# Four layers on one core: operand addresses modulo 256 bytes, and one half of a weight product streamed apart

## The chip, the core and the metric

The kernel runs on one core of a Trainium2 chip. Its time is the device time of one execution in microseconds. The kernel before takes 638.99 us (median of 3 runs, 638.83 to 639.39).

## The reference, cut to what matters

Four layers, each with a residual, work on x of 8 x 256 tokens and 1024 features, all in float32:

```python
x = x + x @ w_eff.T              # L0: weight quantized with a codebook, plus a rank-64 term
x = x + x @ W1.T + 2 * lora(x)   # L1: 8 experts of rank 16, top-2 gates from x @ Wr.T
x = x + x @ W2.T + b + 2 * (x @ A[id]) @ B[id]   # L2: adapter by batch
x = x + x @ W3[id].T             # L3: a whole 1024 x 1024 weight by batch
```

The first three linear parts do not depend on the batch, so the kernel multiplies them together first: E = (I + W0)(I + W1)(I + W2), with the small matrices of the adapters carried along as further columns.

## The kernel before, in words

A float32 number is held as two numbers of type float32r, a high part and the rest. `product` (lines 1259 to 1263) multiplies two such pairs with three matmuls: high by high, high by low, low by high. In `pe.matmul(out, a, b)`, a is the stationary operand of 128 columns, which a weight load puts into the array, and b is the moving one, which streams through it. Each matmul has a weight load of its own; it runs beside the matmul before it.

**First step (about 10 to 127 us).** W1 times the rows of W2. The moving rows are `e_hi` and `e_lo`, the two halves of `e_both` (8 rows of 2 x 1312 numbers; a half is 5,248 bytes). The stationary tiles are W1's columns in two ring buffers, `ring_hi` and `ring_lo`, with room for two tiles. For each of 8 tiles m there are three chunks of 384, 512 and 256 columns; a chunk is `chunk(n)` (line 1333 on): 8 values of k, one product each, 24 matmuls. Between chunks stand `br(c)` (the same product for the adapters, with `bcat_up` and `bcat_down` in rows 7 and 6 of `e_mid` as stationary tiles) and `lora(u)` (the rank-64 term, four matmuls of 256 columns).

**Second step (127 to 239 us).** W0, which DVE and ACT quantize meanwhile in `beat` rounds, times the result. Moving rows: `e_hi` and `e_mid` (8 rows of ES = 1296 numbers, 5,184 bytes). Stationary: the same rings. Three chunks of 384, 512 and 392 columns for each of 8 tiles.

**Four groups of 512 tokens (239 to 635 us).** `low_rank` (moving: `e_both`, stationary: x), then seven `block_product`s of 48 matmuls with 256 columns (moving: x's parts in `x_both`, `x_pair` and both rings, stationary: E's parts in `e_hi`), with the sums and splits of blocks on DVE and ACT. In `gates` (line 1427 on) 16 times four matmuls of 256 columns: `gt_hi` and `gt_lo` (in `bc_hi` and `bc_lo`) move against `br_hi` and `br_lo`, and `h2_k` (in `e_mid`) moves against `bs_half` (in `bc_hi` and `bc_lo`). Then `y_product`, 192 matmuls of 512 columns: W3's parts in `e_hi` move against x's in `e_mid`.

SP issues nearly all loads in program order. PE, ACT, DVE and POOL follow one plan (`phase1_plan`) for the two steps, and written orders (`group`) for the groups. POOL adds the identities to the weights. PE waits on `ring_down` (a tile of a ring is split), `chunk_out` (a bank of PSUM is read out), `delta_out` (the rank-64 term is read out) and `w3_lo` (a half row of W3 is split).

SBUF tensors lie in the order of their declaration. Counted from the start of `e_both`, the bytes of a partition before are: `e_mid` at 83,968, `x_both` at 125,632, `ring_lo` 158,400, `x_pair` 166,592, `ring_hi` 174,784, `raw` 182,976, `bc_hi` 207,552, `bc_lo` 211,648, `br_hi` 215,808, `br_lo` 220,416.

Of the kernel before, what the change touches and what calls it, by code (L numbers as in the profile page):

```python
# [5 lines left out]
F32 = mybir.dt.float32  # L6
F32R = mybir.dt.float32r
# [5 lines left out]
P = 128  # L13
D = 1024
KT = D // P
NB = 8
# [17 lines left out]
ES = EC + 8  # L34
TW = ER + NE + R2
SLOT = [7 if i == 1 else 3 + i // 2 if i % 2 else i // 2 for i in range(NB)]
# [25 lines left out]
N1 = 3 * KT  # L62

# [86 lines left out]
def build(nc, x, cb, lang, id2, id3, w0, scale_log, lora_a, lora_bt, w1, wrt, at, bcat,  # L150
          w2t, b, las, lbs, w3t, y):
    plan = phase1_plan()
    with ExitStack() as ctx:
# [9 lines left out]
        with ExitStack() as whole:  # L163
            def place(name, shape):
                return whole.enter_context(nc.sbuf_tensor(name, shape, F32))
# [5 lines left out]
            ring_lo_w = place("ring_lo_w", [P, 4, 512])  # L171
# [5 lines left out]
        ring_lo = sb("ring_lo", [P, 4, 512], F32R)  # L177
        x_pair = sb("x_pair", [P, 2, D], F32R)
        ring_hi = sb("ring_hi", [P, 4, 512], F32R)
        raw = sb("raw", [P, RAW, D], F32)  # L180
        tmp = sb("tmp", [P, 4, 512], F32)
# [3 lines left out]
        br_hi = sb("br_hi", [P, A0], F32R)  # L185
        br_lo = sb("br_lo", [P, A0], F32R)

        br_now = sb("br_now", [P, 2, 4 * R2], F32R)
        ident = sb("ident", [P, P], F32)
        wr_raw = sb("wr_raw", [P, KT, NE], F32)  # L190
        bias_col = sb("bias_col", [P, KT], F32)
        scales = sb("scales", [P, 2, KT, NE], F32)
        cbs = sb("cbs", [P, 4], F32)
        thr = sb("thr", [P, NL], F32)
        dif = sb("dif", [P, NL], F32)
# [4 lines left out]
        lbias = sb("lbias", [P, NB, NE], F32)  # L200
        lg = sb("lg", [P, 4, NE], F32)
        mx = sb("mx", [P, 4, 4], F32)
        gw = sb("gw", [P, 6, 4], F32)
        oh = sb("oh", [P, 3, 4, NE], F32)
# [6 lines left out]
        scl, rscl = scales[:, 0, :, :], scales[:, 1, :, :]  # L211


# [35 lines left out]
        h2_k = mid[0:96, 8192:8704]  # L249

        tok = mid_w[:, 8704:8704 + 4 * TW].rearrange("p (t c) -> p t c", t=4)
        bs_raw = mid_w[0:96, 8704 + 4 * TW:9728 + 4 * TW]
        h2_tok = scales[:, :, :, :].rearrange("p a k e -> p (a k e)").rearrange("p (t c) -> p t c", t=4)
        h2_sum = mid_w[0:32, 8704:8704 + TG]
        gt_hi, gt_lo = bc_hi[:, 0:TG], bc_lo[:, 0:TG]
        bs_half = [bc_hi[0:96, TG:D], bc_lo[0:96, TG:D]]
# [75 lines left out]
        s_ident = sem("s_ident")  # L332
        s_iota = sem("s_iota")
# [202 lines left out]
        def _(pool):  # L536
# [5 lines left out]
            for j in range(2):  # L542
                pool.memset(br_now[:, j, :].bitcast(F32), 0.0).then_inc(s_ident, 1)
            pool.wait_ge(s_ident, 4)
# [52 lines left out]

            pool.wait_ge(br_down, 3)
# [10 lines left out]
        def _(act):  # L609
# [21 lines left out]
            def split_ring(i, whole):  # L631
# [7 lines left out]
                act.activation(ring(ring_hi, i)[:, ks, :], whole[:, ks, :], ACT.Copy).then_inc(ring_up, 1)  # L639
# [48 lines left out]
            for item in plan:  # L688
# [8 lines left out]
                elif what == "w1_first":  # L697

                    act.wait_ge(s_w1_first, 16)
                    act.activation(ring(ring_hi, 0)[:, 4:KT, :], w1_raw(0)[:, 4:KT, :], ACT.Copy).then_inc(first_up, 1)  # L700
# [187 lines left out]
        def _(dve):  # L888
# [55 lines left out]
            def split_ring(i, whole):  # L944
                dve.wait_ge(ring_up, i + 1)
                ks = slice(0, KT if i else 4)
                minus(ring(ring_lo, i)[:, ks, :], whole[:, ks, :], ring(ring_hi, i)[:, ks, :]).then_inc(ring_down, 1)
# [68 lines left out]
            for item in plan:  # L1016
                what = item[0]
                if what == "w1_first":
                    dve.wait_ge(first_up, 1)
                    minus(ring(ring_lo, 0)[:, 4:KT, :], w1_raw(0)[:, 4:KT, :], ring(ring_hi, 0)[:, 4:KT, :]  # L1020
                          ).then_inc(first_down, 1)
                elif what == "w1_diag":
                    dve.wait_ge(s_w1[0], 16)
                    dve.wait_ge(s_ident, 4)
# [233 lines left out]
        def _(pe):  # L1258
# [46 lines left out]
            def first_chunk():  # L1305
# [3 lines left out]
                for i, kk in enumerate(W2_ORDER[0]):  # L1309
# [269 lines left out]
```

## Time and profile before

| | us |
|---|---|
| median of 3 runs | 638.99 |
| the profiled execution, its own time | 638.79 |
| its span, first to last instruction | 637.0 |
| PE busy | 631.9 |
| DVE busy | 501.4 |
| ACT busy | 364.7 |
| POOL busy | 90.3 |

Times of the rows are counted from the span's start. A matmul's shown duration holds its way through the array, and successive ones overlap, so what one costs is the distance from its start to the start of the next. Where two start times with a known number of matmuls between them are given, their difference over that number is the cost of one.

### The profile page before, as it was taken

Reading aid. Unit: us, or ns where it says so; the run is one execution under the profiler, and the core shown is the slowest. Engines: PE = TensorE matmul, PEld = TensorE weight load, DVE = VectorE, ACT = ScalarE, POOL = GpSimd, SP = SyncE. Lnnn points to the kernel's source line nnn. Section 1 sums busy time; section 2 is a strip of 40 time slices with the busy share of each in tenths; the row PEclk is TensorE's granted clock in tenths of the full one; section 3 lists DMA queues with packets and bytes.
Section 4 is the critical chain, followed back from the end, with each engine's and each line's share of the span. In section 5 each row is a group of like instructions: output and inputs, shape, how many; then the busy total and the mean of one; then the engine's idle time right before and its main releaser. Section 6 shows DMA issues by size and latency. Waiting matters only on the chain.

```text
span 637.0 us, 10326 instructions
## 1 busy us (share of the span) xinstructions
PE 631.9 (99%) x3992; PEld 584.5 (92%) x3992; DVE 501.4 (79%) x645; ACT 364.7 (57%) x549; POOL 90.3 (14%) x120
## 2 busy tenths in 40 slices
PE   8999999999999999999999999999999999999997
PEld 8899999999999999999889999889999889999886
DVE  6899999879991538988887778888687989686753
ACT  6674583972731336745774746665655765664553
POOL 2210225003210010001220001231001223000120
PEclk9999999999999999999999999999999999999999
DMA  8772112111104001213673222684213485002372
GB/s 285 209 206 75 59 33 67 34 33 34 34 0 133 1 1 34 63 64 101 208 253 125 67 67 68 199 261 161 68 34 100 147 283 190 1 1 67 131 245 86
DMA packets 46020, 67.32 MB, mean 106 GB/s; under 512 B 3604, under 2 KB 32020, under 8 KB 45972
## 3 DMA queue, kind: packets, MB, share of 16 engines
q1 hardware_dynamic: 40900, 58.28, 29.0%
q10 hardware_dynamic: 5072, 8.39, 3.8%
q8 instruction: 31, 0.51, 0.4%
q14 instruction: 17, 0.14, 0.1%
HBM read 58.27 MB, written 8.39 MB: 105 GB/s over the span
## 4 chain that ended last, share of the span: by engine, by line
PE 99%; DVE 0%; POOL 0%; issue 0%; POOLq 0%
PE ps L1263 30%; PE ps L1261 30%; PE ps L1262 30%; PE ps L1406 4%; PE ps L1404 1%; PE ps L1272 1%; PE ps L1434 1%; PE ps L1357 1%; PE ps L1450 0%; PE ps L1462 0%; PE ps L1460 0%; PE ps L1442 0%; DVE tmp L1249 0%; DVE tmp L1251 0%; POOL ident L540 0%
## 5 line engine op out<-in xcount | busy, mean ns | idle before, releaser
L1263 PE MATMUL ps<-e_both,ring_lo 128*128 128x384 f32 (+3 forms) x384 | 133.3, 347 | 0.0
L1261 PE MATMUL ps<-e_both,ring_hi 128*128 128x384 f32 (+3 forms) x384 | 133.1, 347 | 0.0
L1262 PE MATMUL ps<-x_both,e_both 128*128 128x256 f32 x448 | 123.7, 276 | 0.0
L899 DVE TENSOR_TENSOR e_both<-raw,e_both 128x512 fp32r<-128x512 f32 x128 | 90.7, 733 | 28.1 <-ACT e_both L773 27.7
L1262 PE MATMUL ps<-e_both,e_mid 128*128 128x512 f32 (+2 forms) x288 | 109.2, 379 | 0.0
L1261 PE MATMUL ps<-e_both,e_mid 128*128 128x512 f32 (+2 forms) x288 | 109.1, 379 | 0.0
L1263 PE MATMUL ps<-e_both,e_mid 128*128 128x512 f32 (+2 forms) x288 | 109.1, 379 | 0.0
L773 ACT ACTIVATE e_both<-raw 128x512 fp32r<-128x512 f32 x128 | 78.8, 628 | 51.5 <-PE ps L1263 51.2
L589 POOL TENSOR_TENSOR raw<-raw,ident 128x128 f32<-128x128 f32 x64 | 47.3, 741 | 338.8 <-DMA raw<-w_t 338.8
L1262 PEld LDWEIGHTS ps<-x_both,e_both 128*128 128x128 f32 x448 | 84.1, 188 | 0.0
L1263 PEld LDWEIGHTS ps<-e_both,ring_lo 128*128 128x128 f32 x384 | 72.1, 188 | 5.5
L1261 PEld LDWEIGHTS ps<-e_both,ring_hi 128*128 128x128 f32 x384 | 72.2, 188 | 5.5
L1262 PE MATMUL ps<-e_mid,ring_hi 128*128 128x384 f32 (+2 forms) x192 | 68.6, 357 | 0.0
L646 ACT ACTIVATE tmp<-tmp,dif 128x1024 f32<-128x1024 f32 x48 | 54.2, 1150 | 18.9 <-DVE tmp L968 15.0
L1262 PE MATMUL ps<-e_both,ring_hi 128*128 128x384 f32 (+2 forms) x192 | 64.5, 336 | 0.0
L970 DVE SCALAR_TENSOR_TENSOR tmp<-w_w,thr,tmp 128x1024 f32<-128x1024 f32 x48 | 60.5, 1303 | 4.2 <-ACT tmp L646 3.8
L1261 PEld LDWEIGHTS ps<-e_both,e_mid 128*128 128x128 f32 x288 | 54.1, 188 | 10.1
L1262 PEld LDWEIGHTS ps<-e_both,e_mid 128*128 128x128 f32 x288 | 54.1, 188 | 10.0
L1263 PEld LDWEIGHTS ps<-e_both,e_mid 128*128 128x128 f32 x288 | 54.1, 188 | 10.0
L899 DVE TENSOR_TENSOR e_both<-e_both_w,e_both 128x1024 fp32r<-128x1024 f32 (+2 forms) x45 | 51.3, 1174 | 10.2 <-ACT e_both L685 7.8
L1261 PE MATMUL ps<-ring_hi,e_both 128*128 128x256 f32 x192 | 53.4, 278 | 0.0
L1263 PE MATMUL ps<-ring_hi,e_both 128*128 128x256 f32 x192 | 53.0, 276 | 0.0
(175 smaller groups left out, 1264.4 us busy)
## 6 DMA issues: line engine op xcount, KB each, us to landing
raw<-w_t SPq DMA_DIRECT2D x64, 512.0 KB, 4.1
w_w<-x_t SPq DMA_DIRECT2D x16, 512.0 KB, 3.8
w_w<-w SPq DMA_DIRECT2D x15, 512.0 KB, 5.3
y<-tmp ACTq DMA_DIRECT2D x30, 256.0 KB, 3.5
e_both_w<-w_t SPq DMA_DIRECT2D x5, 512.0 KB, 7.8
e_both_w<-w_t SPq DMA_DIRECT2D x4, 384.0 KB, 6.0
e_mid_w<-bs SPq DMA_DIRECT2D x24, 64.0 KB, 3.0
e_mid_w<-b_cat SPq DMA_DIRECT2D x4, 128.0 KB, 5.9
```

The costliest lines, as they stand in the source:

```text
L589: pool.tensor_tensor(d, d, ident[:, :], ALU.add).then_inc(w3_diag, 1)
L646: act.activation(acc[i], acc[i], ACT.Identity, bias=dif[:, LEVELS - 1 - level:LEVELS - level]).then_inc(q_add, 1)
L773: act.activation(w3_ring_hi[(2 * k + h) % 4], raw[:, k % RAW, h * 512:(h + 1) * 512], ACT.Copy).then_inc(w3_hi, 1)
L899: return dve.tensor_tensor(out, whole, hi.bitcast(F32), ALU.subtract)
L970: ins = dve.scalar_tensor_tensor(out=acc[i], in0=qf, scalar=thr[:, k:k + 1], in1=acc[i], op0=ALU.is_gt, op1=ALU.mult)
L1261: pe.matmul(out, a[0], b_[0], start=start, stop=False, **kw)
L1262: pe.matmul(out, a[0], b_[1], start=False, stop=False, **kw)
L1263: return pe.matmul(out, a[1], b_[0], start=False, stop=stop, **kw)
L1272: ins = pe.matmul(ps[:, lora_bank(u), 2 * P * i:2 * P * (i + 1)], stack_b[:, b_cols], (stack_a, stack_al)[low][:, a_cols], start=not low a ...
L1357: pe.matmul(ps[:, 7, 0:P], ident[:, :], ident[:, :], start=True, stop=True)
L1404: pe.matmul(ps[:, 4 + t, 0:TW], x_lo[block][:, k % 4, cols], e_hi[:, k, ecols], start=k == 0, stop=False, skip_group_check=True)
L1406: ins = pe.matmul(ps[:, 4 + t, 0:2 * TW].rearrange("p (h c) -> p h c", h=2), x_hi[block][:, k % 4, cols], e_both[:, k, :, ecols], start=Fa ...
```

## The change

- **Middle rows at 5,376 bytes.** ES grows from EC + 8 to EC + 56 numbers: a row of `e_mid` has 5,376 instead of 5,184 bytes. The small tensors `wr_raw`, `scales`, `thr`, `dif`, `lg`, `lbias`, `mx`, `gw`, `oh`, `br_now` and `h2_tok` move into free columns of `e_mid` and `e_both`; `scales` and `wr_raw` are then 8 rows of 32 bytes in each partition. `h2_k` stands 16 numbers further on.
- **Rings.** `ring_hi` and `ring_lo` become 32 numbers longer. W1's and W0's tiles are written and read at `up` and `down`, which begin 32 numbers (128 bytes) into them; x's operands still begin at their start.
- **High and low rows apart.** Chunks 6 to 23 use `chunk_by_halves`: first all 16 matmuls whose moving rows are of `e_hi`, then the 8 of `e_lo`; in chunks of even number the other way round. The number of matmuls is the same.
- **Gates.** `bc_hi` and `bc_lo` become longer, `bs_half` begins 16 numbers further on, and `ids_sb` stands behind `ident`. The places of `gt_hi`, `gt_lo`, `h2_k`, `br_hi`, `br_lo` and `bs_half` follow from that.
- **br_now** is cleared by POOL behind the last chunk with columns 896 on, no longer at the start; PE's first wait is for two updates of `s_ident` instead of four.

```diff
-ES = EC + 8
+ES = EC + 56
+RING_AT = 32
+H2_AT = KT * D + 16
+TOK_AT = H2_AT + TG
+SMALL_AT = TOK_AT + 4 * TW + D
+BY_HALVES = 6
...
-        ring_lo = sb("ring_lo", [P, 4, 512], F32R)
+        ring_lo_all = sb("ring_lo_all", [P, 4 * 512 + RING_AT], F32R)
+        iota_i = sb("iota_i", [P, NE], I32)
+        iota_f = sb("iota_f", [P, NE], F32)
+        lang_i = sb("lang_i", [P, NB], I32)
+        lang_f = sb("lang_f", [P, NB], F32)
         x_pair = sb("x_pair", [P, 2, D], F32R)
-        ring_hi = sb("ring_hi", [P, 4, 512], F32R)
+        ring_hi_all = sb("ring_hi_all", [P, 4 * 512 + RING_AT], F32R)
         raw = sb("raw", [P, RAW, D], F32)
         tmp = sb("tmp", [P, 4, 512], F32)
-        bc_hi = sb("bc_hi", [P, D], F32R)
-        bc_lo = sb("bc_lo", [P, D], F32R)
-        ids_sb = sb("ids_sb", [1, 2, NB], I32)
+        bc_hi = sb("bc_hi", [P, D + 64], F32R)
+        bc_lo = sb("bc_lo", [P, D + 16], F32R)
         br_hi = sb("br_hi", [P, A0], F32R)
         br_lo = sb("br_lo", [P, A0], F32R)
...
+        ring_hi, ring_lo = [of[:, 0:2048].rearrange("p (a c) -> p a c", c=512) for of in (ring_hi_all, ring_lo_all)]
+        up, down = [of[:, RING_AT:2048 + RING_AT].rearrange("p (a c) -> p a c", c=512)
+                    for of in (ring_hi_all, ring_lo_all)]
...
-        bs_half = [bc_hi[0:96, TG:D], bc_lo[0:96, TG:D]]
+        bs_half = [of[0:96, TG + 16:D + 16] for of in (bc_hi, bc_lo)]
...
+            pool.wait_ge(chunk_mm, chunk_number(1, KT - 1, 2) + 1)
+            pool.memset(br_now[:, :, :].bitcast(F32), 0.0).then_inc(br_clear, 1)
+            pool.wait_ge(br_clear, 1)
             pool.wait_ge(br_down, 3)
             pool.wait_ge(e2_down, 4)
             now(0, True)
...
+            def chunk_by_halves(n):
+                _, m, c = CHUNKS[n]
+                c0, w = LEFT[c]
+                pe.wait_ge(ring_down, m + 1)
...
+                out = ps[:, CHUNK_BANK[n], 0:w]
+                parts = [(e_hi, (up, down)), (e_lo, (up,))]
+                for i, (rows, halves) in enumerate(parts if n % 2 else parts[::-1]):
+                    for k in range(KT):
+                        for a, half in enumerate(halves):
+                            ins = pe.matmul(out, ring(half, m)[:, k, :], rows[:, k, c0:c0 + w],
+                                            start=i == 0 and k == 0 and a == 0,
+                                            stop=i == 1 and k == KT - 1 and a == len(halves) - 1)
+                ins.then_inc(chunk_mm, 1)
```

## Rows read from the trace of the kernel before

**Rows 1.** The page: span, PE's busy time and share, granted clock in 40 slices.
```profile
span 637.0 us, 10326 instructions
...
PE 631.9 (99%) x3992; PEld 584.5 (92%) x3992; DVE 501.4 (79%) x645; ACT 364.7 (57%) x549; POOL 90.3 (14%) x120
...
PEclk9999999999999999999999999999999999999999
```

**Rows 2.** PE's waits: us in total, times, longest.
```profile
PE ps L1357 <- POOL br_now L543: 1.6, 1, 1.6
```

**Rows 3.** Timeline of PE, block product: start, duration in us; 29 matmuls apart.
```profile
283.00 0.28 PE L1262 MATMUL ps<-x_both,e_both 128*128 128x256 f32 x1
...
286.29 0.28 PE L1261 MATMUL ps<-bc_hi,br_hi 128*128 128x256 f32 x1
```

**Rows 4.** Timeline of PE, gates and the start of y; 61 matmuls apart.
```profile
286.63 0.28 PE L1434 MATMUL ps<-e_mid,bc_hi 96*128 96x256 f32 x1
...
293.98 0.40 PE L1261 MATMUL ps<-e_both,e_mid 128*128 128x512 f32 x1
```

**Rows 5.** Timeline of PE, y product; 24 matmuls apart.
```profile
304.89 0.39 PE L1261 MATMUL ps<-e_both,e_mid 128*128 128x512 f32 x1
...
310.33 0.39 PE L1261 MATMUL ps<-e_both,e_mid 128*128 128x512 f32 x1
```

**Rows 6.** Timeline of PE, rank-64 term at the start; 14 matmuls apart.
```profile
8.38 0.40 PE L1272 MATMUL ps<-bc_lo,bc_hi 128*128 128x256 f32 x2
...
10.06 0.40 PE L1272 MATMUL ps<-x_pair,bc_hi 128*128 128x256 f32 x2
```

**Rows 7.** Timeline of PE, first step, tile 3: starts and ends of three chunks.
```profile
60.94 0.34 PE L1261 MATMUL ps<-e_both,ring_hi 128*128 128x384 f32 x1
...
65.10 0.40 PE L1272 MATMUL ps<-bc_lo,bc_hi 128*128 128x256 f32 x2
...
65.58 0.39 PE L1261 MATMUL ps<-e_both,ring_hi 128*128 128x512 f32 x1
...
71.10 0.28 PE L1261 MATMUL ps<-e_both,ring_hi 128*128 128x256 f32 x1
...
73.93 0.28 PE L1272 MATMUL ps<-bc_lo,bc_hi 128*128 128x256 f32 x1
```

**Rows 8.** Timeline of PE, second step, tile 6: starts of its chunks and the next.
```profile
211.03 0.34 PE L1261 MATMUL ps<-e_both,ring_hi 128*128 128x384 f32 x1
...
215.22 0.39 PE L1261 MATMUL ps<-e_both,ring_hi 128*128 128x512 f32 x1
...
220.78 0.34 PE L1261 MATMUL ps<-e_both,ring_hi 128*128 128x392 f32 x1
...
225.05 0.34 PE L1261 MATMUL ps<-e_both,ring_hi 128*128 128x392 f32 x1
```

**Rows 9.** Timelines of DVE, ACT and PE where PE's waits end last.
```profile
45.95 1.21 DVE L899 TENSOR_TENSOR ring_lo<-w_w,ring_hi 128x1024 fp32r<-128x1024 f32 x1
...
47.91 0.34 PE L1261 MATMUL ps<-e_both,ring_hi 128*128 128x384 f32 x1
...
102.89 1.09 ACT L618 ACTIVATE raw<-ps 128x512 f32<-128x512 f32 x2 [9.33 <-DVE w_w L979]
...
105.06 0.40 PE L1272 MATMUL ps<-bc_lo,bc_hi 128*128 128x256 f32 x2
...
505.98 1.56 DVE L899 TENSOR_TENSOR e_both<-raw,e_both 128x512 fp32r<-128x512 f32 x2
...
507.22 0.40 PE L1261 MATMUL ps<-e_both,e_mid 128*128 128x512 f32 x1
```

**Rows 10.** DMA issue of scales (KB, us to landing); ACT and DVE behind it.
```profile
scales<-scale_log SPq DMA_DIRECT2D x1, 32.0 KB, 7.6
...
32.58 1.06 ACT L728 ACTIVATE e_both<-w_w 128x1024 fp32r<-128x1024 f32 x1 [3.37 <-DMA w_w<-as]
...
34.62 1.21 DVE L899 TENSOR_TENSOR e_both<-w_w,e_both 128x1024 fp32r<-128x1024 f32 x1
```

More of the change, by code:

```diff
@@ L248, in build @@
         w3_ring_lo = [e_hi[:, 4 + i, 512:D] for i in range(4)]
[L249 to L254, printed above, removed]
+        h2_k = mid[0:96, H2_AT:H2_AT + TG]
+        tok = mid_w[:, TOK_AT:TOK_AT + 4 * TW].rearrange("p (t c) -> p t c", t=4)
+        bs_raw = mid_w[0:96, TOK_AT + 4 * TW:SMALL_AT]
+        h2_sum = mid_w[0:32, TOK_AT:TOK_AT + TG]
         gt_hi, gt_lo = bc_hi[:, 0:TG], bc_lo[:, 0:TG]
[L256 removed]
+        bs_half = [of[0:96, TG + 16:D + 16] for of in (bc_hi, bc_lo)]
         stack_b, stack_a, stack_al = bc_hi, bc_lo, x_pair[:, 1, :]
@@ L541, in _ @@
                                pattern=[[-1, P]], channel_multiplier=1).then_inc(s_ident, 1)
-            for j in range(2):
-                pool.memset(br_now[:, j, :].bitcast(F32), 0.0).then_inc(s_ident, 1)
-            pool.wait_ge(s_ident, 4)
+            pool.wait_ge(s_ident, 2)
             pool.memset(stack_al[R0:P, :].bitcast(F32), 0.0).then_inc(lora_clear, 1)
@@ L638, in split_ring @@
                 ks = slice(0, KT if i else 4)
-                act.activation(ring(ring_hi, i)[:, ks, :], whole[:, ks, :], ACT.Copy).then_inc(ring_up, 1)
+                act.activation(ring(up, i)[:, ks, :], whole[:, ks, :], ACT.Copy).then_inc(ring_up, 1)
             def beat(p, r):
@@ L699, in _ @@
                     act.wait_ge(s_w1_first, 16)
-                    act.activation(ring(ring_hi, 0)[:, 4:KT, :], w1_raw(0)[:, 4:KT, :], ACT.Copy).then_inc(first_up, 1)
+                    act.activation(ring(up, 0)[:, 4:KT, :], w1_raw(0)[:, 4:KT, :], ACT.Copy).then_inc(first_up, 1)
                 elif what == "lora_first":
@@ L946, in split_ring @@
                 ks = slice(0, KT if i else 4)
-                minus(ring(ring_lo, i)[:, ks, :], whole[:, ks, :], ring(ring_hi, i)[:, ks, :]).then_inc(ring_down, 1)
+                minus(ring(down, i)[:, ks, :], whole[:, ks, :], ring(up, i)[:, ks, :]).then_inc(ring_down, 1)
             def beat(p, r):
@@ L1019, in _ @@
                     dve.wait_ge(first_up, 1)
-                    minus(ring(ring_lo, 0)[:, 4:KT, :], w1_raw(0)[:, 4:KT, :], ring(ring_hi, 0)[:, 4:KT, :]
+                    minus(ring(down, 0)[:, 4:KT, :], w1_raw(0)[:, 4:KT, :], ring(up, 0)[:, 4:KT, :]
                           ).then_inc(first_down, 1)
@@ L1379, in _ @@
             for n in range(1, 2 * N1):
-                chunk(n)
+                if BY_HALVES <= n < N1:
+                    chunk_by_halves(n)
+                else:
+                    chunk(n)
                 if n in BR_AFTER:
```

62 lines of the change are left out of this document (38 added, 24 removed).

## The prediction

> **What bounds the kernel now.** I read the page first: PE is busy for 631.9 of the 637.0 us of the span, and its granted clock is at the full level (2.4 GHz) in all 40 slices [rows 1]. Then the list of PE's waits: it has one entry, 1.6 us ahead of the first warm-up matmul [rows 2]. So no transfer and no other engine ends anything; the time is the sum of the distances between 3,992 matmul starts. The question is what one matmul costs, and for that I read start times far apart.
>
> Block product: 29 matmuls of 256 columns from 283.00 to 286.29, 113.4 ns each [rows 3]. Y product: 24 of 512 columns in 5.44 us, 226.7 ns each [rows 5]. The second is twice the first, 0.4427 ns a column, where 2.4 GHz alone would be 0.4167. I call this the base: 113.3 ns for 256 columns, and by the same slope 170.0 for 384 and 173.5 for 392. Now the others. Gates: the first three matmuls, 286.29 to 286.63, are at base; the next 61 of the same size take 7.35 us, 120.5 ns each [rows 3, 4]. Rank-64 term at the start: 14 in 1.68 us, 120.0 ns [rows 6]. First step, tile 3: 4.16 us for 24 of 384 (173.3 ns), 5.52 for 24 of 512 (230.0), 2.83 for 24 of 256 (117.9) [rows 7]. Second step, tile 6: 4.19, 5.56 and 4.27 us, or 174.6, 231.7 and 177.9 ns [rows 8]. Equal shapes on equal clock differ by up to 7 ns, without any wait.
>
> What differs is addresses. From the order and sizes of the tensors I work out each operand's phase: its address modulo 256 bytes, from the start of e_both. A row of e_both has 10,496 bytes, 41 times 256, and its half 5,248, so e_hi has phase 0 and e_lo 128; column offsets 384 and 896 are whole multiples.
>
> - Block product: moving x's parts, all 192; stationary 0. Moving phase constant, stationary minus moving 64. Base.
> - Y product: both 0, constant, difference 0. Base.
> - Gates: gt_hi and gt_lo 192 against br 0, then h2_k 0 against bs_half 192: the moving phase turns twice in four matmuls. The slow stretch begins with the first h2_k.
> - First step: moving 0, 128, 0; stationary 192. Second: e_hi 0, e_mid's row k at 64k (5,184 is 64 over a multiple); stationary 192. Off base.
> - Rank-64 term: both 192, constant, and yet 6.7 ns over base.
>
> So a constant moving phase with a difference of 64 runs at base, a turning one does not, and constancy alone is not enough. That is the reading on which I forecast.
>
> **The change part by part.** All sums are against the profiled execution, 638.79 us (span 637.0 and 1.8 around it), 0.2 below the median 638.99.
>
> *Gates.* New phases from the new sizes: gt_hi, gt_lo and h2_k 64, br and bs_half 128. Constant, difference 64, 256 columns: the case of the block product. 61 matmuls x 7.2 ns is 0.44 us, four groups 1.76. At the least nothing; I take 1.7, as a turn remains at either end.
>
> *Second step.* A row of 5,376 bytes is 21 times 256, so e_mid has phase 0 like e_hi; the rings go from 192 to 64. Constant, difference 64. Over base now: 4.19 - 4.08 = 0.11, 5.56 - 5.44 = 0.12, 4.27 - 4.16 = 0.11 us a tile. Eight tiles: 1.84 for the first two chunks and 0.86 for the third. The block product shows the rule for 256 columns only, but 384 and 512 are also whole multiples of 64 bytes. 392 is not: its last piece is half of one, and I take half of that chunk's gain, 0.43. For the turn of size at 24 chunk starts I give back 0.01 each: the y product needs 1.39 us for its first six instead of 1.36 when it follows the gates (its start is the last of [rows 4]), which is 0.03 for a turn of phase and size together. 1.84 + 0.43 - 0.24 = 2.0 us. Bounds: 0 and 2.7.
>
> *First step, chunks 6 to 23.* 12.51 us a tile against 12.24 at base [rows 7], so 0.27 a tile, 1.64 for six. By halves, the 16 matmuls of e_hi have moving 0 and stationary 64, the good case; the 8 of e_lo have 128 against 64, a difference of 192, which before occurs only mixed with others. Between 0 and the rank-64 term's 6.7 ns for each of those; I take 4.5, near the mean overrun now (0.27 us / 72 = 3.8 ns). 8 x 4.5 + 10 for the turn is 46 ns a chunk; 18 chunks keep 0.83 and give 0.8 us. Bounds 0.3 and 1.64.
>
> *Chunks 0 to 5, br, the rank-64 term.* The order is as before with other phases; two of three matmuls of a ring product now have a difference of 64, before one of three. br's stationary tiles go to phase 0, the rank-64 term to 64 against 64 and 192. Nine chunks' worth of products, about 90 ns over base each, 0.8 us, and 64 matmuls of the term with up to 0.43. I take a gain of 0.1; bounds +0.5 and -1.2 us.
>
> *low_rank, block products, y product.* Both operands keep their phases: x's parts stay at 192 (32,768, 8,320 + 128 bytes and so on keep it), E's and W3's at 0. Nothing.
>
> *Start.* PE's first wait goes from L543's end to that of the identity, 0.2 to 0.3 us earlier, but warm-up is all that moves; the rank-64 term waits for DVE's split of data from a DMA. Nothing. br_now is cleared while DVE still splits the last columns; POOL then waits for them anyhow. Nothing.
>
> *Small tensors.* scales and wr_raw arrive in runs of 32 bytes instead of 256, 1,024 instead of 128. The load of scales now takes 7.6 us to land in a queue full of W2; ahead of the adapters, whose landing lets ACT start at 32.58. ACT is done at 33.64 and DVE comes for it at 34.62 [rows 10], so up to 0.9 us more costs nothing. Beyond it DVE's chain slips, and PE has 0.75 us to its next ring tile (45.95 + 1.21 = 47.16 against 47.91 [rows 9]). I take 0; the bound is half a microsecond.
>
> *What is late next.* PE comes earlier, and others don't. Tile 2 of the ring has 0.75 us, of which chunks 0 to 5 can use some tenths. The rank-64 unit that PE takes at 105.06 waits for ACT at 102.89 + 0.6 = 103.5 [rows 9], 1.5 us, and ACT waits for DVE there; PE will be 0.7 to 1.2 us early. In the third group W3's half row is split at 505.98 + 0.7 + some hundredths, 506.95, and PE takes it around 507.2 [rows 9]: that is almost bound, by x's transfers. With gates 0.44 us shorter it can cost 0.2 once. I take 0.2 in all.
>
> Sum: 1.7 + 2.0 + 0.8 + 0.1 - 0.2 = 4.4 us; 638.79 - 4.4 = 634.4.
>
> Rows against a page: matmuls alike in shape take 113.4 and 120.5 ns within one microsecond of each other [rows 3, 4]. The Trainium skill (TensorE: Matmul & The Clock Gate, Part 2, the step on LDWEIGHTS) says that PE has two independent read ports and that loading the next weights takes nothing from the running matmul; by that no address could matter and the sum would be 0, the third rival. The same page (Back-to-back issue gap) gives N / 2.4 + 2.5 ns, 109.2 for 256 columns by its formula, an estimate that no row here reaches. The measurement decides against both as written, though not on why.
>
> **The rivals.**
>
> 1. *All at base.* The halves of e_lo and the 392 columns run clean too, and the early products gain. 1.76 + 2.7 + 1.64 + 0.9 = 7.0, so 631.8. For it: y runs clean with another difference (0). Against: the rank-64 term doesn't.
>
> 2. *Only part holds.* The difference 64 helps at 256 columns as shown, longer ones or e_lo keep most of their overrun: gates 1.7 and a third of the two steps' 4.3 make 3.1 less 0.2, or only the gates 1.7. 635.9 to 637.1. For it: in the second step rows k = 0 and 4 of e_mid already have e_hi's phase and the chunks are still off base, though with difference 192.
>
> 3. *The addresses are not the cause.* Something in the alternation of tensors or banks is. The change then does not do what it says; 638.8, with 0.2 either way. Against it stands the break in the gates after three matmuls.
>
> 4. *Slower: the new constant phases lock into the bad pattern.* The rank-64 term shows that a constant pair can cost 6.7 ns for every matmul without end. If the rings at 64 do that, 42 chunks x 24 = 1,008 matmuls pay 6.7 us over base, where they now pay 1.64 + 2.7 = 4.3: 2.4 us more, 641.2. It decides from 4.3 ns a ring matmul on. The place is the two steps; the gates, at 6.7 instead of 7.2, would be even. Against: 64 is the block product's difference, not the term's.
>
> **How the numbers follow.** The forecast 0.53, with a range of its own of 633.0 to 635.8; all at base 0.12; part 0.18; no cause in addresses 0.09; slower 0.08. 0.2% is 1.3 us, about what a measurement of this kernel can tell from no change. Faster by more (below 637.7): the first two and nearly all of the third, 0.82. Within: 0.10, the fourth and a rest of the third. Slower: 0.08. The range 631.5 to 637.6 leaves out the last two cases and the edges.
>
> **What would show it.** In the changed trace: gates of 113 to 114 ns a matmul, a group's 61 in 6.9 us; second step, tile 6, 4.08, 5.44 and 4.16 to 4.27 us; in a chunk by halves the e_hi part at 170.0, 226.7 and 113.3 ns and the e_lo part above it; block and y products unchanged to the nanosecond. Wrong would be: chunks with constant phases that stay at 174 or 231 ns (rival 3) or go beyond (rival 4); any entry of microseconds in PE's list of waits, at a ring tile, delta_out or w3_lo; a clock below 1.0.

## The result, and the profile after

The changed kernel takes 640.79 us (median of 9 runs, 640.65 to 640.95) against 638.99 (9 runs): a ratio of 1.0027, 95% interval 1.0019 to 1.0035. It is slower by 1.8 us where 4.4 us less were forecast, and lies outside the forecast range. The page and the list of PE's waits:

```profile
span 639.0 us, 10325 instructions
...
PE 634.1 (99%) x3992; PEld 585.3 (92%) x3992; DVE 500.4 (78%) x645; ACT 364.9 (57%) x549; POOL 96.9 (15%) x119
...
PEclk9999999999999999999999999999999999999999
```

```profile
PE ps L1403 <- POOL ident L564: 1.4, 1, 1.4
```

No work has moved between engines; POOL is busy 6.6 us longer, but of PE's waits only the first is put down to it. As in [rows 1, 2] PE is busy from end to end at full clock; what differs is the price of a matmul. PE's timeline in the second step's tile 6 (start, duration; the chunks begin 24 matmuls apart), which answers to [rows 8]:

```profile
212.36 0.34 PE L1287 MATMUL ps<-e_both,ring_hi_all 128*128 128x384 f32 x1
...
216.60 0.39 PE L1287 MATMUL ps<-e_both,ring_hi_all 128*128 128x512 f32 x1
...
222.20 0.34 PE L1287 MATMUL ps<-e_both,ring_hi_all 128*128 128x392 f32 x1
...
226.52 0.34 PE L1287 MATMUL ps<-e_both,ring_hi_all 128*128 128x392 f32 x1
```

4.24, 5.60 and 4.32 us, or 176.7, 233.3 and 180.0 ns a matmul: each size is 6.5 to 6.7 ns (about 16 cycles) over the forecast's base. Before, [rows 8] gave 174.6, 231.7 and 177.9.

The same timeline from the end of the block products over the gates into y, which answers to [rows 3 to 5] (29, 48, 3 and 61 matmuls apart, and 24 between the last two):

```profile
279.17 0.28 PE L1289 MATMUL ps<-ring_hi_all,e_both 128*128 128x256 f32 x1
...
282.46 0.28 PE L1287 MATMUL ps<-ring_hi_all,e_both 128*128 128x256 f32 x1
...
288.11 0.28 PE L1287 MATMUL ps<-bc_hi,br_hi 128*128 128x256 f32 x1
288.47 0.28 PE L1483 MATMUL ps<-e_mid,bc_hi 96*128 96x256 f32 x1
...
295.69 0.40 PE L1287 MATMUL ps<-e_both,e_mid 128*128 128x512 f32 x1
...
302.98 0.39 PE L1289 MATMUL ps<-e_both,e_mid 128*128 128x512 f32 x1
...
308.42 0.39 PE L1289 MATMUL ps<-e_both,e_mid 128*128 128x512 f32 x1
```

The 29 ahead of 282.46, the h2 sum's four at their end, still take 113.4 ns each. From 282.46 to 288.11 stand the 48 matmuls of the last block product: 117.7 ns each, where the forecast (and [rows 3]) has 113.4 with the same operand addresses. Gates: 7.58 us for 64, against 7.69 before. Y: 24 in 5.44, as before.

All stages, from such start times (us; the four groups summed; the last column is from e15 below; the 4.05 us behind the last row are alike in all three):

| stage | before | changed | difference | best version |
|---|---|---|---|---|
| first matmul of the first step starts at | 10.30 | 9.95 | -0.35 | 9.84 |
| first step | 116.60 | 117.45 | +0.85 | 117.31 |
| second step | 112.18 | 113.28 | +1.10 | 111.35 |
| low_rank and all but the last block product | 165.23 | 165.25 | +0.02 | 165.22 |
| h2 sum and last block product | 23.58 | 24.46 | +0.88 | 23.57 |
| gates | 30.78 | 30.30 | -0.48 | 29.01 |
| y, 192 matmuls of each group | 170.50 | 170.54 | +0.04 | 170.55 |

In the first step 0.53 us are two short waits of PE that the list of waits does not show, 0.25 us inside the first chunk and 0.28 at ring tile 2: DVE begins its split at 46.87, not 45.95 [rows 9], and PE, there at about 47.9, takes the tile at 48.14 (DVE's row, then PE's).

```profile
46.87 1.21 DVE L925 TENSOR_TENSOR ring_lo_all<-w_w,ring_hi_all 128x1024 fp32r<-128x1024 f32 x1
```

```profile
48.14 0.45 PE L1395 MATMUL ps<-e_both,ring_hi_all 128*128 128x384 f32 x1
```

### The profile page after: what moved, and what is told of

Its sections match the earlier page's. It is cut to its first block, busy times and chain, and to the rows that moved or that the text cites. A ratio compares the mean times of both kernels' runs of the same rounds, so it can differ in the third digit from the quotient of the medians.

```text
span 639.0 us, 10325 instructions
## 1 busy us (share of the span) xinstructions
PE 634.1 (99%) x3992; PEld 585.3 (92%) x3992; DVE 500.4 (78%) x645; ACT 364.9 (57%) x549; POOL 96.9 (15%) x119
## 4 chain that ended last, share of the span: by engine, by line
PE 99%; DVE 0%; POOL 0%; issue 0%; POOLq 0%
PE ps L1287 26%; PE ps L1288 26%; PE ps L1289 26%; PE ps L1395 12%; PE ps L1455 4%; PE ps L1453 1%; PE ps L1298 1%; PE ps L1483 1%; PE ps L1403 1%; PE ps L1499 0%; PE ps L1511 0%; PE ps L1509 0%; PE ps L1491 0%; DVE tmp L1275 0%; DVE tmp L1277 0%
## 5 line engine op out<-in xcount | busy, mean ns | idle before, releaser
L611 POOL TENSOR_TENSOR raw<-raw,ident 128x128 f32<-128x128 f32 x64 | 49.7, 779 | 335.7 <-DMA raw<-w_t 335.7
L1287 PE MATMUL ps<-e_both,ring_hi_all 128*128 128x384 f32 (+3 forms) x240 | 84.9, 354 | 0.0
L1289 PE MATMUL ps<-e_both,ring_lo_all 128*128 128x384 f32 (+3 forms) x240 | 84.8, 354 | 0.0
L1395 PE MATMUL ps<-e_both,ring_hi_all 128*128 128x384 f32 (+2 forms) x288 | 72.3, 337 | 0.0
L1288 PE MATMUL ps<-e_mid,ring_hi_all 128*128 128x384 f32 (+2 forms) x192 | 68.7, 358 | 0.0
L672 ACT ACTIVATE tmp<-tmp,e_mid_w 128x1024 f32<-128x1024 f32 x48 | 54.2, 1151 | 19.3 <-DVE tmp L994 15.4
L996 DVE SCALAR_TENSOR_TENSOR tmp<-w_w,e_mid_w,tmp 128x1024 f32<-128x1024 f32 x48 | 60.3, 1299 | 4.2 <-ACT tmp L672 3.8
L571 POOL TENSOR_TENSOR w_w<-w_w,ident 128x128 f32<-128x128 f32 x15 | 33.8, 2263 | 136.8 <-DVE w_w L1005 81.8
L1395 PEld LDWEIGHTS ps<-e_both,ring_hi_all 128*128 128x128 f32 x288 | 50.1, 188 | 4.3 <-DVE ring_lo_all L925 0.2
L1287 PE MATMUL ps<-ring_hi_all,e_both 128*128 128x256 f32 x192 | 53.7, 279 | 0.0
L1289 PE MATMUL ps<-ring_hi_all,e_both 128*128 128x256 f32 x192 | 53.3, 278 | 0.0
```

The lines of the kernel that those rows point to most:

```text
L571: return pool.tensor_tensor(d, d, ident[:, :], ALU.add)
L611: pool.tensor_tensor(d, d, ident[:, :], ALU.add).then_inc(w3_diag, 1)
L672: act.activation(acc[i], acc[i], ACT.Identity, bias=dif[:, LEVELS - 1 - level:LEVELS - level]).then_inc(q_add, 1)
L996: ins = dve.scalar_tensor_tensor(out=acc[i], in0=qf, scalar=thr[:, k:k + 1], in1=acc[i], op0=ALU.is_gt, op1=ALU.mult)
L1287: pe.matmul(out, a[0], b_[0], start=start, stop=False, **kw)
L1288: pe.matmul(out, a[0], b_[1], start=False, stop=False, **kw)
```

## The experiments

"Difference" is stationary minus moving phase, modulo 256 bytes; "excess" is what a matmul takes over base (17 cycles for 16 columns at 2.4 GHz); a matmul or a stretch without it is called clean. Theory A is the forecast's rule. Theory B: size and difference fix a few possible values of the excess, and what PE did just before picks one, which then stays. In its first form (e1 to e3) B had three values for all sizes, 0, about 4.5 and 6.7 ns; the 3.3 and 2.2 ns that e1 shows made them more.

**e1: PE alone.** A kernel with matmuls and nothing else, `RUNS.append(run(m, s, n))` over four sizes, four moving and four stationary phases.

> Computes none of the layer: PE alone, 77 runs of matmuls between drains, zeros as operands. 60 matmuls of 512 columns, then 20 matmuls for each of 256, 384, 512, 392 columns x moving phase 0, 64, 128, 192 x stationary phase 0, 64, 128, 192; then twelve runs of 12 matmuls of 256 columns (moving 0, stationary 64), one other matmul, and 24 more of the first kind. Theory A (the forecast's rule): the runs with stationary minus moving 64 take the base (113.3, 170.0, 226.7, 173.5 ns a matmul), those with 192 lie above it, whatever came before. Theory B (a stretch of equal matmuls keeps the excess with which it was entered): the excess per matmul is one of a few values (0, about 4.5, 6.7 ns), the same difference of phases shows more than one of them over the four sizes, and one other matmul in between can turn a run of 0 into a run of 4.5 or 6.7 that lasts for its remaining 24. Theory C (addresses have no part): all 16 pairs of a size alike.

The 16 pairs of a size fall into classes by difference. ns a matmul over the last 12 of a run:

| columns | base | 0 | 64 | 128 | 192 |
|---|---|---|---|---|---|
| 256 | 113.3 | 120.0 | 113.3 or 117.8 | 118.8 or 120.0 | 117.8 |
| 384 | 170.0 | 173.3 | 173.3 or 174.6 | 176.3 | 173.3 |
| 512 | 226.7 | 226.7 once settled | 233.3 | 231.7 to 233.3 | 228.9 |
| 392 | 173.5 | 177.1 to 177.6 | 177.8 or 180.0 | 175.5 | 179.4 to 180.0 |

The base of 384 and of 392 columns is worked out from the other two sizes; no pair reaches it. The runs go through the eight banks of PSUM in turn, so the pairs of one difference lie in different banks and are still alike: the bank has no part in it.

PE's timeline in it. A row holds the two or three matmuls under way at one moment (x2, x3) and begins with the start of the first; the rows of a pair lie 12 matmuls apart: first 256 columns at difference 0 (27.54, 28.98) and 64 (30.26, 31.62), then 512 columns at 0 (132.16, 134.88) and 64 (137.06, 139.86).

```profile
27.54 0.52 PE L59 MATMUL ps<-mv,st 128*128 128x256 f32 x3
...
28.98 0.52 PE L59 MATMUL ps<-mv,st 128*128 128x256 f32 x3
...
30.26 0.50 PE L59 MATMUL ps<-mv,st 128*128 128x256 f32 x3
...
31.62 0.50 PE L59 MATMUL ps<-mv,st 128*128 128x256 f32 x3
...
132.16 0.62 PE L59 MATMUL ps<-mv,st 128*128 128x512 f32 x2
...
134.88 0.61 PE L59 MATMUL ps<-mv,st 128*128 128x512 f32 x2
...
137.06 0.63 PE L59 MATMUL ps<-mv,st 128*128 128x512 f32 x2
...
139.86 0.63 PE L59 MATMUL ps<-mv,st 128*128 128x512 f32 x2
```

1.44 against 1.36 us, but 2.72 against 2.80: the difference that is best at 256 columns is the dearest at 512. A falls, and so does C (addresses have no part). Of the twelve runs with an odd matmul in the middle, several leave for the other value of their pair and stay there for the remaining 24: one of other phase turned 113.3 into 117.8, one with 32 columns of weights turned it back.

**e2: no halves.** `-BY_HALVES = 6` / `+BY_HALVES = 24` in the changed kernel.

> The changed kernel with every chunk of the first step in the old order (high, low, high row for each k), phases as changed. Theory A: each chunk's e_lo matmuls stand between e_hi ones at other phases, first step longer by up to 1 us, second step unchanged at 14.16 us a tile. Theory B (history): the second step is entered from other matmuls, so its excess of 16 cycles a matmul need not stay: 13.68 (none), 14.0 (10.7 cycles) or 14.16 us a tile; the first step within 1 us of before's. If the halves are what made it slower, the total falls under 639.0.

640.50 us, 1.0019 (1.0008 to 1.0030) of before. First step 117.42 us against 117.45, chunks 6 to 23 alone 79.17 against 79.26: the halves gain nothing and cost at most 0.1. The second step began at 14.03 us in its first tile, 14.11 in the second and 14.16 from the third on; the same addresses have several values, and the kernel drifts into the dearest. (The changed kernel is there from the first tile.)

**e3: rings back.** `up, down` at `of[:, 0:2048]`, phase 192.

> The changed kernel with the ring's W tiles at the phase of x's operands (192, as before the change), all else as changed: e_mid's rows stay at phase 0. Theory A: difference 192 in the second step, above base, 14.0 to 14.2 us a tile; chunks by halves e_lo part at difference 64 and at base, e_hi part off it. Theory B: an excess of its own, constant over the eight tiles since all phases are constant: 13.68, 14.0 or 14.16 us a tile. Everything after the second step as in the changed kernel if the history is forgotten there, gates 7.57 us a group.

638.84 us, 0.9992 (0.9981 to 1.0003). Tile 6:

```profile
210.99 0.34 PE L1287 MATMUL ps<-e_both,ring_hi_all 128*128 128x384 f32 x1
...
215.15 0.39 PE L1287 MATMUL ps<-e_both,ring_hi_all 128*128 128x512 f32 x1
...
220.65 0.34 PE L1287 MATMUL ps<-e_both,ring_hi_all 128*128 128x392 f32 x1
...
224.95 0.34 PE L1287 MATMUL ps<-e_both,ring_hi_all 128*128 128x392 f32 x1
```

4.16, 5.50 and 4.30 us, or 173.3, 229.2 and 179.2 ns, near e1's column for 192; 13.95 a tile, a value that neither theory had named. This one edit takes 1.63 us off the changed kernel's second step (111.65 against 113.28), more than all it had lost there.

**e4: another place for br_now.** `-br_now = small(mid, 0, ...)` / `+br_now = small(mid, 48, ...)`, with `mx`, `gw`, `oh` and `h2_tok` moved to fit.

> The changed kernel with one small tensor moved: br_now starts 192 bytes further on, so that in the h2 sum (four small matmuls ahead of the last block product) its moving phase is 0 and the stationary 64. The last block product has the same addresses in both. Theory A (its own phases decide): no change, 118.0 ns for each of its 48 matmuls, as in the changed kernel. Theory B (the state in which it is entered decides): it can return to the 113.3 ns that it had before the change, 0.22 us a group and 0.9 us in all, and the gates behind it may change with it, by up to 0.5 us a group either way. Total 639.9 to 640.8.

640.06 us, 1.0013 (1.0002 to 1.0025). The expectation misnames the h2 sum's phases: from the declarations gt_hi and gt_lo move at 64, and br_now, stationary, goes from 192 to 128; the difference is 64, as it says. The h2 sum and last block product take 5.940 us a group (6.115 changed, 5.893 before), though the block product's own operands have not moved:

```profile
282.05 0.28 PE L1287 MATMUL ps<-ring_hi_all,e_both 128*128 128x256 f32 x1
...
287.52 0.28 PE L1287 MATMUL ps<-bc_hi,br_hi 128*128 128x256 f32 x1
```

5.47 us instead of 5.65 for the 48. After five matmuls of turning it is at 113.3. Here the state at entry decides, not the phases of the stretch.

**e5 and e6: sequences, and finer steps.** PE alone again, now in the kernel's order and sizes; and stationary phases in steps of 16 bytes, offsets over 256, other sizes.

> Computes none of the layer: PE alone, in the order and sizes of the kernel's stretches, zeros as operands, drains between runs. For each of four phases of W: three tiles of the second step (24 matmuls of 384, 24 of 512, 24 of 392, all rows at phase 0); the first step in the old order and by halves, rows of e_lo at 128, and once more with them at 0; and a block product, 64 gate matmuls and 12 of y for five pairs of gate phases. Theory B1 (difference of phases and size together decide, history only chooses among a few values): second step per tile from the single-shape runs, difference 0: 173.4 + 226.7 + 177.0 ns, x 24 = 13.85 us; 64: 14.03 at first and up to 14.16 later; 128: 175.4 + 232.1 + 175.6, 14.0; 192: 173.4 + 228.9 + 180.0, 13.97 (13.95 in the kernel with the rings back). Theory C2 (something of the real kernel, other engines' traffic or banks, makes the +16 cycles of the second step): here 64 stays at 14.03 us in all three tiles. Gates: (64, 128) 118 ns on average as in the changed kernel, others not forecast.

> Computes none of the layer: PE alone, zeros as operands. 24 equal matmuls between drains for stationary phases 0, 16, ..., 240 against moving phase 0, at 256, 384, 512 and 392 columns; then stationary offsets of 256 to 2112 bytes at 256 and 512 columns; then seven other sizes at four phases. If the period is 256 bytes, offsets that are whole multiples of 256 behave as 0 (120.0 ns at 256 columns, 226.7 at 512) and 320, 576, 1088, 2112 as 64 (113.4 or 117.8; 233.4). If 64 bytes is the grain, 16, 32 and 48 behave as 0 or as 64; if it is finer there are new values, perhaps a phase at base for 384 columns, for which none of the 16 pairs so far was under 173.2 ns.

Three tiles of the second step at difference 64: 14.02 (without its entry), 14.11, 14.16 us, the very drift of e2; at 0, 13.92; at 128, 14.02; at 192, 13.95. No other engine runs here, so theory C2 falls: the order of the matmuls alone makes it. In e6 offsets of 256, 512, 1,024 and 2,048 behave as 0 and those 64 further as 64, which fits a period of 256 bytes; below 64 there are new values, but none of 16 phases brings 384 columns under 173.3 ns. 128 and 192 columns both take 111.7 ns.

e5 also has 24 matmuls of a block product (192 against 0) and 64 of the gates' size behind them, all of 128 rows. With the gates at 192 against 0 as well they take 113.3 ns. With the changed kernel's 64 against 128, the same difference, they are entered at 113.3 ns and take 117.8 all the same, 7.538 us for 64. Starts 12 matmuls apart in the block product (516.07, 517.43), then 48 apart in the gates (518.83, 524.48):

```profile
516.07 0.62 PE L68 MATMUL ps<-mv,st 128*128 128x256 f32 x4
...
517.43 0.62 PE L68 MATMUL ps<-mv,st 128*128 128x256 f32 x4
...
518.83 0.63 PE L68 MATMUL ps<-mv,st 128*128 128x256 f32 x4
...
524.48 0.63 PE L68 MATMUL ps<-mv,st 128*128 128x256 f32 x4
```

So a turn to another pair of the same difference is enough to lose the clean state.

**e7: rings at phase 0.** e4 with `up, down` at `of[:, 16:2048 + 16]`.

> The changed kernel with two placements moved: the ring's W tiles at phase 0 instead of 64, and br_now 192 bytes further on as in e4. Theory B1: second step at difference 0, 24 x (173.4 + 226.7 + 177.0) = 13.85 us a tile against 14.16, 2.5 us in all; the h2 sum and last block product 5.94 us a group as in e4, 0.7 us; first step: e_hi parts at difference 0 (173.4, 226.7, 120.0 ns), e_lo parts at 128 (175.4, 232.1, 118.1), within 0.7 us of the changed kernel. Total 637.0 to 638.0. Theory A (difference 64 is the good one, at every size): second step slower than 14.16 us a tile, total above 640.

638.35 us, 0.9986 (0.9977 to 0.9996), above the 637.0 to 638.0 expected. Tile 6:

```profile
210.92 0.33 PE L1287 MATMUL ps<-e_both,ring_hi_all 128*128 128x384 f32 x1
...
215.10 0.39 PE L1287 MATMUL ps<-e_both,ring_hi_all 128*128 128x512 f32 x1
...
220.58 0.34 PE L1287 MATMUL ps<-e_both,ring_hi_all 128*128 128x392 f32 x1
...
224.84 0.33 PE L1287 MATMUL ps<-e_both,ring_hi_all 128*128 128x392 f32 x1
```

13.92 us a tile, 0.07 over the sum from e1; e5 has that 0.07 too (the first matmuls after each turn of size).

**e8: fewer columns of weights.**

> Computes none of the layer: PE alone, zeros as operands. Runs of 24 matmuls of 256, 384 and 512 columns with 128, 96, 64 and 32 columns of weights at the four differences of phase; then runs of 40 at difference 64, each entered from 12 matmuls of another kind. Theory D (the excess over 17 cycles per 16 columns is a meeting of the next weights' load with the moving operand's reads): fewer columns of weights, less excess, at 32 columns at most a third of what 128 columns show (16 cycles at 512 columns, difference 64), while the 17 cycles per 16 columns stay. Theory E (it is set by the moving operand alone, or at the border between matmuls): the same excess for any number of weight columns. Entered four ways: at 256 columns both 113.4 and 117.8 ns occur, at 384 173.4 and 176.6, at 512 always 233.4.

Neither D nor E. At 256 columns and 32 of weights three of the four differences are clean; but at 512 columns difference 0 goes from 226.7 (128 columns of weights) to 230.0 (96, 64) and 231.7 (32). The number of weight columns takes part, yet fewer are not always better. What exactly meets what stays open. The entries show B again: 256 columns at 64 ran at 117.8 ns behind two of the four kinds and settled at 113.3 behind the others, to the end of the 40; 384 at 173.3 or 174.6 to 174.8, 512 always at 233.3.

**e9: the gates alone, in the kernel before.** `-h2_k = mid[0:96, 8192:8704]` / `+h2_k = mid[0:96, 9840:10352]`, and `bs_half` 16 numbers on: 192 against 0 throughout.

> The kernel before, with the gates alone changed: h2_k moved to phase 192 and the two halves of bs to phase 0, so that moving 192 against stationary 0 holds from the last block product through all 64 gate matmuls (first rows of the kernel before: 192 against 0 for gt and br, 0 against 192 for h2_k and bs). Theory B: the state without excess, which the block products have, is kept: 113.3 ns a matmul, 7.25 to 7.3 us a group against 7.69, 1.6 to 1.8 us in all; total 637.2 to 637.5. Theory A gives the same, since the difference is 64. If the gates come out at 117.8 ns (the other state of the same pair), 7.54 a group and 0.6 us in all.

638.62 us, 0.9988 (0.9973 to 1.0003). 7.557 us a group, not 7.25: a miss for A and B. Three matmuls are clean, and from the fourth on the cycles over base repeat as 9, 18, 14, 6. So the phases were made constant and the break stayed where it was; they are worth 0.14 us a group, 0.55 in all.

**e10 and e11.** e7 with `bc_hi`, `bc_lo`, `br` and `h2_k` 128 bytes further on (192 against 0 as in e9); then also `scales = sb("scales", [P, 2, KT, NE], F32)`.

> As e7 (rings at phase 0), with bc, br and h2_k 128 bytes further on: moving 192, stationary 0 from the block products through the h2 sum and the gates, without a turn. h2 sum and last block product 5.893 us a group as before the change (5.940 in e7), gates 7.25 to 7.3 against 7.577; 1.4 us less than e7 in all: 636.8 to 637.2. If the state of the gates is set by something else, they stay at 7.57 us.

> As e10, with the scales in a tensor of their own (128 runs of 256 bytes in their load instead of 1,024 of 32). If the small packets are what sets DVE back by 0.9 us (46.9 us for the split of ring tile 2 instead of 46.0), then in this kernel it starts at 46.0 to 46.3 again and PE's wait of 0.29 us at 48 us goes: 0.2 to 0.4 us less than e10. If the delay comes from elsewhere (PE's earlier start, the landings of W2), no difference.

638.02 us (0.9977, 0.9962 to 0.9992) and 638.08. Last block product 5.893 us a group, as expected; gates 7.557, as in e9 and not the 7.25 to 7.3 expected, so the total is a miss by 1 us. In e11 DVE splits ring tile 2 at 45.68, in e10 at 45.26, and e9, whose loads are those of the kernel before, has 47.36 and a wait of PE of 0.1 us at the same tile. So the early waits come and go from execution to execution; the packets of 32 bytes do not make them.

**e12: rows.** What distinguishes the fourth gate matmul is in its row, above and in [rows 4]: `96*128 96x256`. PE alone, patterns of contracted rows.

> Computes none of the layer: PE alone, zeros as operands. Per difference of phase (64, 0, 128, 192) and pattern of contracted rows (all 128; 128, 128, 128, 96 as in the gates; 128, 128, 128, 64; all 96; all 64; all 32): 20 matmuls of 256 columns with 128 rows, 64 in the pattern, 20 with 128 rows. Then 512 and 384 columns; then the h2 sum's four matmuls (64, 32, 64, 32 columns of weights) in a clean stretch at four pairs of phases. Theory F (the 96 rows are what breaks the clean state): pattern 128, 128, 128, 96 gives 118.1 ns at difference 64 with the period of four of e9, all 128 gives 113.3 when entered clean. Theory G (the tensors or banks of the gates do it): rows make no difference, 113.3 or 117.8 in every pattern of difference 64.

256 columns, difference 64: all 128 rows 113.3 ns; 128, 128, 128, 96 in turn 118.3; all 96 113.3. The three were not entered alike: the 20 matmuls of 128 rows ahead ran at 113.3 ns in the first and at 117.8 in the other two. PE's timeline, the rows of a pair 44 matmuls apart, first the mixed pattern, then all 96 (granted clock 1.00 in both; it fell only in the runs with 32 rows):

```profile
42.16 0.52 PE L59 MATMUL ps<-mv,st 128*128 128x256 f32 x3
...
47.36 0.52 PE L59 MATMUL ps<-mv,st 128*128 128x256 f32 x3
...
73.41 0.50 PE L59 MATMUL ps<-mv,st 96*128 96x256 f32 x3
...
78.40 0.50 PE L59 MATMUL ps<-mv,st 96*128 96x256 f32 x3
```

Theory F holds as far as it goes: not few rows, but their change goes with 118.3 ns; what it does to a clean entry, e13 tests. At difference 192 the change costs 1.4 ns (119.2 against 117.8), at 0 and 128 nothing (120.0 and 118.3 against 120.0 and 118.6). Far dearer is 128, 128, 128, 64 in turn, 215.0 to 216.7 ns a matmul at every difference. The h2 sum's four matmuls inside a stretch of 192 against 0: with (moving, stationary) at (64, 192), the changed kernel's pair, the stretch ran at 113.3 ns ahead of them and at 117.8 behind; at (0, 64) it went from 117.8 to 113.3; at (128, 64) and (192, 192) it stayed at 113.3 and 117.8.

**e13: 128 rows in the gates.** e10, with

```diff
-                    ins = pe.matmul(tile_of(bank, m), bs_half[o][:, m * P:(m + 1) * P], h2_k[:, ts],
+                    ins = pe.matmul(tile_of(bank, m), bs_all[o][:, m * P:(m + 1) * P], h2_all[:, ts],
```

and rows 96 to 127 cleared once by POOL.

> As e10, with the fourth matmul of the gates contracting 128 rows instead of 96: rows 96 to 127 of h2_k and of the two halves of bs are cleared once, the result is the same. Theory F: the clean state of the block product goes on through the gates, 113.3 ns a matmul, 7.25 us a group against 7.557 in e10, 1.2 us in all; total 636.6 to 637.0. Theory G: 7.557 us as before, total 638.0.

637.18 us, 0.9972 (0.9961 to 0.9983). Gates 7.253 us a group, 113.3 ns each, as F says, with the same clean entry as in e10: the 96 rows made the break. But the first group's block products take 33.956 us instead of 33.210. PE's timeline there; the first and last pairs are 24 matmuls apart:

```profile
249.48 0.28 PE L1295 MATMUL ps<-x_pair,e_both 128*128 128x256 f32 x1
...
252.20 0.28 PE L1295 MATMUL ps<-ring_hi_all,e_both 128*128 128x256 f32 x1
...
257.52 0.28 PE L1297 MATMUL ps<-ring_hi_all,e_both 128*128 128x256 f32 x1
257.67 0.36 PE L1295 MATMUL ps<-ring_lo_all,e_both 128*128 128x256 f32 x1
...
266.22 0.28 PE L1295 MATMUL ps<-ring_lo_all,e_both 128*128 128x256 f32 x1
...
269.05 0.28 PE L1295 MATMUL ps<-x_pair,e_both 128*128 128x256 f32 x1
```

2.72 us for 24 ahead of a wait of 0.11 us at 257.5, 2.83 behind it: matmuls of equal shape and equal phases. The small wait moved PE into the other state, for 144 matmuls. My clearing had held up POOL's additions of the identity, which in e10 begin at 233.81 and take 1.72 us for four; here they begin at 240.64 and took 5.54:

```profile
238.88 0.52 POOL L636 MEMSET e_mid<- 32x512 f32 x1 [4.84 <-PE ps L1297]
...
240.64 5.54 POOL L614 TENSOR_TENSOR raw<-raw,ident 128x128 f32<-128x128 f32 x4
```

**e14: all combinations for the second step.**

> Computes none of the layer: PE alone, zeros as operands. e_hi at phase 0; the middle rows, the high and the low W tile each at 0, 64, 128 or 192: 64 combinations, each 24 matmuls of 392, 384, 512 and 392 columns in the kernel's order; then the first step with e_lo at 128 and 16 combinations of the two W tiles, 256, 384, 512 and 256 columns. If only differences of neighbouring operands count, the constant combinations give 13.92 (0), 14.03 to 14.16 (64), 14.04 (128) and 13.95 us (192) for the last three chunks as in e5, and mixed ones lie among them; if some mixed one keeps the clean state at 384 and 392 columns too, it lies at 13.68 to 13.8.

Of 64, all at 0 is the lowest, 13.73 us for the three chunks (71 distances); the rest lie between 13.77 and 13.94, all at 64 at 13.92. No mixed one is clean at 384 or 392 columns. For the first step the 16 lie between 12.41 and 12.62.

**e15: the clearing later.** e13, with POOL's clearing behind its first four additions.

> As e13, but POOL clears the 32 rows after its first four additions of the identity instead of ahead of them. In e13 PE met a wait of 33 + 80 ns at 257.5 us of the span and ran the next 144 matmuls of the block product at 117.8 ns instead of 113.3, 0.64 us. Theory B: without the wait the first group's products take 33.210 us again (33.956 in e13), gates stay at 7.253; total 636.4, 0.7 to 0.8 us under e13. If the wait comes from elsewhere it stays, total 637.2.

636.47 us, 0.9960 (0.9947 to 0.9974), as expected to 0.1: faster than both kernels. The wait is gone; block products 33.210, gates 7.254:

```profile
285.69 0.28 PE L1297 MATMUL ps<-bc_hi,br_hi 128*128 128x256 f32 x1
286.03 0.28 PE L1493 MATMUL ps<-e_mid,bc_hi 128*128 128x256 f32 x1
...
292.95 0.39 PE L1297 MATMUL ps<-e_both,e_mid 128*128 128x512 f32 x1
```

**e16: the changed kernel with 128 rows only.**

> The changed kernel with 128 rows in the gates' fourth matmul (the other 32 rows are zeros) and nothing else. Its last block product runs at 118.0 ns. Theory B (the state is carried over): the gates' 64 matmuls stay at 117.8 ns, 7.54 us a group against 7.575, total 640.6. If rows and phases alone decide (the forecast's rule, mended by the rows): 113.3 ns, 7.25 us a group, total 639.5.

640.44 us, 1.0021 (1.0012 to 1.0030). Gates:

```profile
287.67 0.28 PE L1297 MATMUL ps<-bc_hi,br_hi 128*128 128x256 f32 x1
288.02 0.28 PE L1493 MATMUL ps<-e_mid,bc_hi 128*128 128x256 f32 x1
...
295.21 0.40 PE L1297 MATMUL ps<-e_both,e_mid 128*128 128x512 f32 x1
```

7.54 us, 117.8 ns: 128 rows and a constant difference of 64 are not enough. Two things are left that e15 has otherwise, and e16 does not part them: the entry, at 117.7 ns here, and the turn from 192 against 0 to 64 against 128. In e5 the same turn gave the same 7.54 us from a clean entry, so the turn alone suffices.

## Why the prediction was wrong

**What bounds the kernel** held in the main: PE's distances are the time, but for 0.53 us of waits, and equal shapes differ by amounts that stay. The base of 0.4427 ns a column holds for 256 and 512 columns only: the 170.0 and 173.5 ns for 384 and 392 are reached in no run, the lowest in e1, e6 and e14 are 173.3 and 175.5.

**The step that failed** is the sentence "So a constant moving phase with a difference of 64 runs at base". It was read from one size. e1 shows that the best difference depends on the columns. The rows had already said so: y at difference 0 ran at base with 512 columns [rows 5], the rank-64 term at difference 0 was 6.7 ns over with 256 [rows 6]. I took that as "constancy alone is not enough" where the other thing that differed was the size.

- *Second step*, forecast -2.0, bounds 0 and -2.7; measured +1.10. "384 and 512 are also whole multiples of 64 bytes" carried a rule for 256 columns over to sizes where 64 gives 173.3 to 176.7 and 233.3 ns. A loss was not within the bounds, though no row excluded one. e3 undoes it (13.95 us a tile), e7 betters it (13.92). Since 384 and 392 columns don't come down to the base, even the best version gains only 0.83 of the 2.7 that the forecast took for the most.
- *Gates*, forecast -1.7; measured -0.48. The phases came out as worked out, and no matmul of the changed gates is clean. The row of the break [rows 4] carries its cause in plain sight, 96 rows beside 128; I gave it to the phases because both changed at the same matmul. e9 separates them, and e10 against e13 shows the rows. The phases, held at the block product's own 192 against 0, are worth 0.55 us (e9), the rows 1.21 more (e13), together 1.76 (30.78 to 29.01). That this is near the forecast's 1.7 is luck: it was forecast for the phases alone, and for 64 against 128, which e5 and e16 show not to be clean behind the block product.
- *Block products*, forecast 0; measured +0.88, all in the last one. Its operands kept their phases, as said. The h2 sum ahead of it did not (192 against 0 before, 64 against 192 after), and it leaves PE in another state. The forecast priced every stretch by its own addresses; e4 and e12 show that the stretch ahead counts.
- *First step, chunks 6 to 23*, forecast -0.8; measured +0.15 (79.26 us against 78.99, less 0.11 of the wait at tile 2). *Chunks 0 to 5*, forecast -0.1; +0.16 without waits. The e_hi part, 16 of 24 matmuls at difference 64, came out at 173.4 to 176.6, 233.5 and 113.4 to 117.8 ns for the three sizes, where 170.0, 226.7 and 113.3 were forecast: dear at 512 columns above all. e16, with the changed kernel's phases and without these waits, has 79.14 us for chunks 6 to 23. Of the 0.15 streaming apart has at most 0.1 (e2).
- *Start*, forecast 0; it began 0.35 earlier here and up to 0.3 later in other executions, and the waits that follow vary with it. *Small tensors*, forecast 0: right, by e10 and e11. *Waits late next*, forecast 0.2: 0.53 in this execution, one of the two at the ring tile that was named.

The rivals: the third, that addresses are not the cause, falls with e3, where moving the rings alone takes 1.63 us off the second step. The fourth ("the new constant phases lock into the bad pattern", 641.2 us, chance 0.08) was nearest, 0.4 off. Its price, 6.7 ns a ring matmul, is what all 576 of the second step pay, to 0.2 ns; in the first step they do not, and the block product, which it left out, pays instead, and 0.53 us are waits: that the total comes so near is in part luck. Its chance was too small because the one argument against it was again the block product's 256 columns.

The Trainium skill (TensorE: Matmul & The Clock Gate, Back-to-back issue gap) gives N / 2.4 + 2.5 ns for a matmul in isolation, by my estimate 215.8 for 512 columns, and about 131 ns for each of a stream with weight loads. Both are under e1's 226.7 to 233.3, which decides. The Trainium skill (TensorE: Matmul & The Clock Gate, LDWEIGHTS, loading the stationary operand) puts a load at P / 1.2 for P columns. The trace agrees on the slope: in e8 loads of 32, 64, 96 and 128 columns show 108, 134, 162 and 189 ns, 0.84 ns a column, with a constant on top. By my estimate P / 1.2 is 107 ns for 128; e6's floor of 111.7 ns for 128 and 192 columns is near it, though no run shows that the load sets it.

## What to carry to other kernels

Where PE is never idle, read the price of a matmul from start times, by size, by rows contracted and by what ran just before, and do not carry a value from one of these to another: the same pair of addresses cost 113.3 or 117.8 ns, and with a wait of 0.11 us a stretch took 0.75 us more. When two things change at the same instruction, look at every column of its row before naming one of them. A stretch of equal matmuls and nothing else, one run for all sizes and phases, would have shown the rule false before the change was made.

## What the hardware showed

- At 256 and 512 columns float32r matmuls come down to 17 cycles for 16 columns, 113.3 and 226.7 ns; 384 and 392 don't (173.3 and 175.5 at best), and 128 costs as much as 192 (111.7). On top come up to 7.6 ns a matmul (512 columns, difference 96) in patterns that repeat over one to seven matmuls. They depend on the stationary minus the moving address modulo 256 bytes and on the columns (e1, e6).
- The same operands have two steady prices at 256 columns and difference 64, 113.3 and 117.8 ns, and up to three values in the second step's sequence. An odd matmul, a turn of size or of phases, or a short wait moves PE between them (e1, e2, e5, e8, e13).
- At difference 64, contracting 96 rows in every fourth matmul ends the clean state of all four, 118.1 ns against 113.3 (e10, e13); 96 in all costs nothing; 64 in every fourth makes it 215 ns (e12).
- Which reads meet which, and why 256 bytes, no run here tells.
